# Loading the odd row blocks of four matrix passes through the second DMA queue

## The reference

```python
x = ln(x + (adj @ (x @ W0) + b0))                                   # L0
x = ln(x + relu(concat(x, adj @ x / max(rowsum(adj), 1)) @ W1.T))   # L1
# L2, two iterations: V = x @ Wv + bv;  edge = adj.T @ V;  att = softmax((x @ Wq + bq) @ edge.T * s * adj)
#     masks from att and from cosine similarity prune adj; two products with the pruned matrix follow
x = ln(x + L2(x, adj))
# L3: w = mask(adj) * 0.5 ** (distance from the row's end, at most 100 neighbours);  out = w @ (x @ W3) + b3
x = ln(x + L3(x, adj))
```

## Time and profile before

| | |
|---|---|
| median of 3 runs | 2545.32 us (2545.17 to 2545.76) |
| profiled execution | 2542.96 us, span 2541.2 us |
| TensorE busy | 2064.3 us (81%) |
| VectorE busy | 1772.7 us (70%) |
| ScalarE busy | 784.8 us (31%) |
| moved by DMA | 838.27 MB, mean 330 GB/s |
| granted TensorE clock, mean | 0.915 |

### The profile page before, as it was taken

One profiled execution on the slowest core, in us unless ns is written; L12 is line 12 of the kernel. 1 busy time (PEld: TensorE's weight loads), 2 busy tenths in 40 slices (PEclk: granted clock), 3 DMA queues, 4 the chain that ended last, 5 costly groups with the idle time before them and its releaser, 6 DMA issues. The chain is left out here.

```text
span 2541.2 us, 37390 instructions
## 1 busy us (share of the span) xinstructions
PE 2064.3 (81%) x15632; PEld 728.4 (29%) x15632; DVE 1772.7 (70%) x2037; ACT 784.8 (31%) x992; POOL 4.1 (0%) x16
## 2 busy tenths in 40 slices
PE   6788869799966666589999989977656669996898
PEld 2223233223221111133344323221111123333333
DVE  7875964088778888865544148869888875554898
ACT  0001011066633233311111026643323221111797
POOL 0000000000000000000000000000000000000000
PEclk9999989999978787789999999988878779998999
DMA  9967979989759989977769979948989896774696
GB/s 385 423 288 293 428 319 424 403 310 381 269 227 364 375 356 365 385 281 280 280 233 387 428 298 377 378 152 357 368 363 363 356 363 253 280 280 178 263 420 260
DMA packets 123763, 838.27 MB, mean 330 GB/s; under 512 B 8544, under 2 KB 10592, under 8 KB 76640
## 3 DMA queue, kind: packets, MB, share of 16 engines
q1 hardware_dynamic: 121424, 833.68, 82.6%
q10 hardware_dynamic: 2192, 2.40, 0.3%
HBM read 699.73 MB, written 136.31 MB: 329 GB/s over the span
## 5 line engine op out<-in xcount | busy, mean ns | idle before, releaser
L873 DVE CUSTOM_DVE_ANT_0 stream<-ps,stream 128x1024 f32<-128x1024 f32 x504 | 594.4, 1222 | 132.4 <-DMA stream<-in_adj 90.3
L884 ACT ACTIVATE stream<-stream,negmax 128x4096 f32<-128x4096 f32 x128 | 475.1, 3712 | 592.8 <-DVE negmax L878 592.8
L840 PE MATMUL ps<-edgeT,node_twice 64*128 64x512 f32 x1024 | 293.6, 697 | 248.2 <-DVE mx L873 248.2
L426 PE MATMUL ps<-stream,stage 128*64 128x512 f32 x1792 | 402.9, 600 | 55.6 <-DMA stream<-in_adjT 29.5
L1211 DVE SCALAR_TENSOR_TENSOR stream<-stream,cut 128x4096 f32<-128x4096 f32 x62 | 278.0, 4484 | 6.2
L840 PE MATMUL ps<-edgeT,query_twice 64*128 64x512 f32 x1024 | 246.8, 615 | 6.4 <-DVE edgeT L904 4.0
L1171 PE MATMUL ps<-stream,xw 32*64 32x512 f32 x4096 | 224.9, 589 | 2.4 <-issue 1.8
L840 PEld LDWEIGHTS ps<-edgeT,node_twice 64*128 64x128 f32 x1024 | 98.4, 209 | 438.8 <-DVE mx L873 323.2
L426 PEld LDWEIGHTS ps<-stream,stage 128*64 128x64 f32 x1792 | 126.8, 138 | 323.8 <-issue 250.5
L855 PE MATMUL ps<-stream,ones 128*1 128x512 f32 x1024 | 182.2, 849 | 11.2 <-DVE stream L1211 11.2
L1389 DVE SCALAR_TENSOR_TENSOR query_twice<-stream,query_twice 128x512 bf16<-128x512 f32 x256 | 154.6, 686 | 4.5 <-ACT query_twice L1367 4.5
(11 more groups left out here) (189 smaller groups left out, 1444.6 us busy)
## 6 DMA issues: line engine op xcount, KB each, us to landing
stream<-in_adj SPq DMA_DIRECT2D x178, 2048.0 KB, 11.7
stream<-in_adjT SPq DMA_DIRECT2D x74, 2048.0 KB, 13.1
pruned<-stream SPq DMA_DIRECT2D x64, 2048.0 KB, 7.5
spare<-pruned SPq DMA_DIRECT2D x22, 2048.0 KB, 11.0
query_twice<-pruned SPq DMA_DIRECT2D x22, 2048.0 KB, 11.3
node_twice<-pruned SPq DMA_DIRECT2D x20, 2048.0 KB, 11.5
query_twice<-in_adjT SPq DMA_DIRECT2D x7, 2048.0 KB, 34.8
node_twice<-in_adjT SPq DMA_DIRECT2D x7, 2048.0 KB, 34.8
```

What stands on the lines that cost most here:

```text
L426: last = nc.tensor.matmul(ps[F * h:F * h + F, bank + b, :], stage[:, t.k % SL, :], half_bank(src, b, h), start=False, stop=False, skip_gro ...
L840: last = nc.tensor.matmul(ps[:, 2 * slot + h, :], stationary[F * h:F * h + F, rows_n], bank_of(edgeT[F * h:F * h + F, :], c), start=True, ...
L873: nc.vector.tensor_tensor_reduce(out=prod[s][:, cols], in0=ps[:, 2 * slot:2 * slot + 2, :].rearrange("p a b -> p (a b)"), in1=block_in[:, ...
L884: nc.scalar.activation(prod[s], prod[s], ACT.Exp, bias=negmax[:, s:s + 1], accum_out=zsum[:, s:s + 1]).then_inc(exp_done, 1)
```

## The change

In `accumulate`, SyncE issues only the blocks of even step number. ScalarE issues those of odd number: the first ones (1, 3, 5 and, with eight slots, 7, unless resident or already issued) before it waits for the features, the later ones inside its loop, behind the wait on `used` (and one on `added` where VectorE reads the blocks) and ahead of the copy into `stage`. Sizes, slots and semaphores stay.

```diff
@@ -387,7 +387,7 @@
             @block.sync
             def _(sp):
                 def body(t):
-                    if t.k < max(resident, issued):
+                    if t.k < max(resident, issued) or t.k % 2 == 1:
                         return
                     wait(sp, used, t.n - (SL - 1))
                     if on_vector:
@@ -397,10 +397,18 @@
 
             @block.scalar
             def _(act):
+                if not resident:
+                    for k in range(SL):
+                        if k % 2 == 1 and k >= issued:
+                            act.dma_start(slot[slots[k]], matrix_b[seq[k]]).then_inc(loaded[k], 16)
                 act.wait_ge(*moved_ready)
 
                 def body(t):
                     wait(act, used, t.n - (SL - 1))
+                    if t.k % 2 == 1 and t.k >= max(SL, resident):
+                        if on_vector:
+                            wait(act, added, t.n - (SL - 1) - first_on_vector)
+                        act.dma_start(slot[slots[t.k % SL]], matrix_b[t.block]).then_inc(loaded[t.k % SL], 16)
                     nc.scalar.activation(stage[:, t.k % SL, :], natural_block(moved, t.block), ACT.Copy)\
                         .then_inc(staged, 1)
                     if t.it is None and t.k in scalar_side:
```

## The result

The changed kernel took 2588.24 us (median of four runs, 2587.22 to 2591.61) against 2545.24 us beside it: a ratio of 1.0173, 95% interval [1.0156, 1.0191], 43 us slower. That is under 2%, but far outside the interval of no change. Predicted were 2586 us and +42. Its profiled execution has a span of 2586.2 us, 45.0 more than before.

A forecast was written before the change was run, and what follows sets the result against it. DMA transfers were taken to bound the edge passes and `l0` to block 24, then TensorE, and VectorE `l1`. 10 + 0 + 24 + 8 = +42 us on 2543.0 gave 2585, stated as 2586 near the runs' median; range 2560 to 2608.

The forecast's parts named there:

- Bandwidth, 0: Data-bound loads: two busy queues move 434 GB/s, 1% more than 429; nothing taken, ends 0 and 4 us.
- `l1`, 0: Pass `l1`: VectorE stays the bound and loads come well ahead of use; 0 us, ends 0 and +2.
- `l0`, +10: Pass `l0`: `xT` shares turns with odd blocks, later odd loads lag behind small loads; +10 us, ends -3 and +15.
- `i0_edge`, +24: Pass `i0_edge`: later first odd loads, idle DMA while ScalarE is held, later end; +24 us, ends +12 and +32.
- the prologue's 7.2: Start of `i0_edge`: loads 1, 3, 5 go out only behind ScalarE's copies and leave the shadow; +7.2 us.
- the holds' 13.7: `i0_edge`: `make_starts` holds ScalarE, so loads 9 and 11 go out late and DMA engines idle; +13.7 us.
- The end of the edge passes, +2.4 to +4.8 each: Last blocks: 29 and 30 land together, 31 one load later, so TensorE ends later behind the last landing.
- `i1_edge`, +8: Pass `i1_edge`: `roots` holds load 11, DMA gaps of 6.1 us plus an end of 2.4; +8 us, ends +2, +13.
- The waits foretold: TensorE waits: about 11 us before blocks 9 and 11 in `i0_edge`, 5 to 8 before block 11 in `i1_edge`.
- harmless-`l0` rival: Queue start of `l0` costs 0 to +4 us, 2573 to 2580; chance 0.19 below 2570, shared with cheaper holds.
- the cheap-holds rival: Edge passes lose little beyond the late first loads; +7 to +20 us, 2552 to 2565; shared chance 0.19.
- the faster one: Data-bound loads: two queues move more bytes, break-even at 4.38 us a load, 2530 us at 4.2; chance 0.05.

The follow-up runs named there:

- late odd loads only: Kernel of before, but in both edge passes ScalarE issues the odd loads from block 13 on: ratio 1.0026, +6.6 us.
- the one-block experiment: Kernel of before, but in `l0` ScalarE issues only block 1 ahead: first projection at 15.17 us; single run 2546.47 us against 2546.32.
- the pair of experiments: Change in `l0` alone: ScalarE's first loads wait for `xT` and `W0`, 1.0053; or ScalarE issues only blocks 1, 3, 5, 7, 1.0006.
- the switch-over kernel: Kernel of before, but in `l0` ScalarE issues the odd loads from block 21 on: ratio 1.0034, +8.7 us.
- the last kernel above: Kernel of before, but the second half of `xT` is issued from ScalarE's queue, all block loads by SyncE: ratio 0.9992.

## Why the prediction was right

- **Bandwidth, 0.** Right: block pairs 9.8 us apart where both queues are full, 2 x 4.89, and the edge passes with late odd loads only are slower.
- **`l1`, 0.** Right: +0.5 [-1.8, +2.8] alone.
- **`l0`, +10.** The chain of steps was right and 2 to 5.5 us small: first copy 37.73 for 34.8, block 9 at 82.07 for 76.6, block 25 at 155.49 for 153, end 195.2 for 193. Most of it is the first step: 21.1 us of delay where 18.2 were worked out; the one-block experiment puts 1.2 us on top once and 4.98 rather than 4.55 (18.2 / 4) for each block. That the late features are absorbed and the late odd loads are not is shown by the pair of experiments. That only the lag behind the small loads could do it is not so: the switch-over kernel lost +8.7 by passing in front.
- **`i0_edge`, +24, measured 20.** The step that failed is the division into two terms, the prologue's 7.2 and the holds' 13.7. The experiments show 0 for the prologue while the holds stand (+20.9 against +20.4), and 10 less with two of the held loads taken away. In the prediction's own walk transfers begin again at 430.3 with 19 loads and the store to do, whatever went before: 430.3 + 92.9 + 2.5 = 525.7, 18.8 behind 506.88, where the two terms had made 20.9 of it. With an end of 2.4 to 4.8 that is +21 to +24; load 11 went out 1.2 us sooner than worked out (441.46 less the 15.0 by which the pass began later, for 427.6). Measured from the start of the phase, the last block landed 18.4 us later than before, and the end cost 1.5: +20.
- **The end of the edge passes, +2.4 to +4.8 each (3 and 2.4 taken).** Too large. TensorE ended 5.3 and 4.8 us behind the last landing in the changed kernel, for 3.8 before: +1.5 and +1.0. With late odd loads only it was +1.1 and +2.4. The walk has block 31 land a whole load after 30; in the changed `i0_edge` it landed 1.9 us after it, because it had shared its turns with 30. The 4.4 and 4.7 us of the experiment fit the term only because a hold is in them.
- **`i1_edge`, +8.** 6.9 in the profile, 5.9 of it by the later last landing, where gaps of 6.1 had been worked out; 6.4 [3.8, 8.9] alone. The wait before block 11 was 8.73 us, and 8.16 in the pass alone, for 5 to 8.
- **The waits foretold.** 11 us before block 9 was 7.48, as load 9 went out 1.8 us earlier than worked out (see the first point on the hardware below) and its sharing was shorter. Before block 11 it was 12.48. Of the 2.8 us by which block 9 was there sooner, 1.6 were lost again before load 11, since block 9 itself ran slower (the last point below).
- The harmless-`l0` rival is refuted by the pass alone (+15.5), the cheap-holds rival by the +20.4 and +6.4 of the edge passes, against +7 to +20 for both, and the faster one by the changed kernel and by every kernel that puts block loads in both queues: none of them is faster.

The change within 1 us of the forecast is partly luck: `i0_edge` was 4 too high, `l0` 3 too low, and `l1` and the stretch between the edge passes, put at 0, were 2.3 and 3.6 longer. With the change in `i0_edge` alone that stretch took 837.7 us, as long as in the changed kernel, but it also took 836.8 in the last kernel above, whose `i0_edge` is that of before. So the 3.6 us may be scatter, and it stays open.

## What to carry to other kernels

A DMA put on a compute engine's queue inherits every wait that stands ahead of it in that engine's program; list these waits with their releasers before moving it, and price the idle of the DMA engines that each leaves, not the wait of the consumer. Two queues that share the DMA engines turn by turn, as here, land blocks out of the order of their use: keep loads that are used in order in one queue, and bulk loads out of the way of small rows. When several losses fall before one fixed moment (here the release of a side job), count what is left to transfer after it instead of adding them.

## What was not expected of the hardware

- ScalarE issued a DMA while activations that stand ahead of it in program order were still to run; the waits between them were met. Load 9 was issued at 421.59 us, while the first of four activations ahead of it had started at 421.58 and the last ended at 424.0.
- SyncE's issues of two 16 KB loads took 21.53 us while `xT` crept through its turns (1.97 us before, and 8.05 with one block beside `xT`), so a queue that drains slowly holds its issuing engine as well.
- TensorE's clock was lower around its long waits: in the change of `i0_edge` alone the granted clock was 0.75 on the mean over 410 to 440 us, so about half of that time at 1.2 and not 2.4 GHz, around the waits before blocks 9 and 11, and 1.00 in the 26 us ahead of them; in the changed kernel block 9 took 5.26 us after its wait of 7.48 us, not 3.65. That is not free here: the count behind block 9 releases the second `make_starts` and with it load 11, and the DMA engines stand partly idle until then, so these 1.6 us are part of the hole.
